# Chunkwise attention over eight heads at once: masks in the exponent matmul, exponents one half-batch ahead, row normalisation moved to ScalarE

## The reference

```python
q = layernorm(x);  k = v = ctx                         # per head
D[s,t] = exp(g[t] - max_{u<=s} g[u])  for t <= s, else 0   # g: input gate minus the summed log forget gate
C = (q @ k.T / sqrt(32)) * D
C = C / (max(|sum(C)|, exp(-m)) + 1e-6)
h = C @ v;  h = head_layernorm(h) * outnorm_weight
x = x + h
x = x + moe(layernorm(x))     # 8 experts, top 2 of them for each token, silu(h1) * h2
```

## Time and profile before

| | us |
|---|---|
| time before, median of 3 runs | 697.69 (697.56 to 697.80) |
| the profiled execution's own time | 699.08 |
| its span | 697.0 |
| TensorE busy | 599.0 |
| VectorE busy | 479.0 |
| ScalarE busy | 315.7 |
| GpSimd busy | 306.7 |

### The profile page before, as it was taken

The page is one execution under the profiler, slowest core; times in us unless marked ns, Lnnn a source line. Parts: engine busy times, 40 slices in busy tenths (PEclk is TensorE's granted clock), DMA queues, the critical chain, the costliest instruction groups (busy, mean ns, idle before and its releaser), DMA issues.

```text
span 697.0 us, 14852 instructions
## 1 busy us (share of the span) xinstructions
PE 599.0 (86%) x3480; PEld 465.8 (67%) x3481; DVE 479.0 (69%) x1039; ACT 315.7 (45%) x704; POOL 306.7 (44%) x312
## 2 busy tenths in 40 slices
PE   3874499999999997411799999999999999999993
PEld 1331266676667665311588888888888888888883
DVE  3663447778787887899367676767677676767673
ACT  2454344545445453100455555555555555555551
POOL 2223435463645545000355454555555454555532
PEclk9998599999999999555799999999999999999997
DMA  8995545556564653351132433333332333333332
GB/s 272 294 305 170 176 134 158 177 171 180 164 196 156 174 166 105 104 205 8 39 63 47 62 49 58 53 54 53 54 61 46 62 49 58 53 54 56 51 46 24
DMA packets 71673, 76.77 MB, mean 110 GB/s; under 512 B 12830, under 2 KB 63780, under 8 KB 71652
## 3 DMA queue, kind: packets, MB, share of 16 engines
q1 hardware_dynamic: 55652, 50.27, 23.0%
q0 software_dynamic: 15712, 25.73, 20.3%
q10 hardware_dynamic: 288, 0.52, 0.2%
HBM read 53.29 MB, written 23.21 MB: 110 GB/s over the span
## 4 chain that ended last, share of the span: by engine, by line
PE 71%; DVE 15%; DMA 5%; issue 3%; ACT 2%; SPq 1%; POOL 1%; DVEq 0%; ACTq 0%; POOLq 0%
PE bank L1270 10%; PE bank L1272 10%; PE bank L1271 9%; PE bank L1168 6%; PE bank L1184 6%; PE bank L1302 5%; PE bank L1298 5%; PE bank L1299 5%; PE bank L1285 4%; DMA qT_scratch<-qt 3%; PE bank L1257 2%; PE bank L1233 2%; PE bank L1165 2%; PE bank L1163 2%; DVE ohn L934 2%
## 5 line engine op out<-in xcount | busy, mean ns | idle before, releaser
L1090 POOL DMA_INDIRECT out_rows<-ys,index x71 | 113.5, 1599 | 153.7 <-DVE ys L986 145.2
L1270 PE MATMUL bank<-w12l,xh 128*128 x284 | 120.3, 424 | 2.2 <-DVE xl L958 2.2
L1272 PE MATMUL bank<-w12h,xh 128*128 x284 | 112.4, 396 | 0.0
L1271 PE MATMUL bank<-w12h,xl 128*128 x284 | 112.2, 395 | 0.0
L992 DVE TENSOR_TENSOR w3l<-w,w3h 128x1024 fp32r<-128x1024 f32 x71 | 87.2, 1228 | 31.0 <-issue 30.0
L1081 POOL DMA_INDIRECT xg<-token_table,index x71 | 70.5, 993 | 74.9 <-DVE index L951 53.0
L1184 PEld LDWEIGHTS bank<-aug,c 128*128 128x128 f32 x512 | 67.1, 191 | 29.9 <-issue 24.4
L656 ACT CAST w3h<-w 128x1024 fp32r x71 | 74.4, 1048 | 20.0 <-issue 20.0
L1298 PE MATMUL bank<-w3l,hth 128*128 128x256 f32 x284 | 76.5, 302 | 1.8 <-DVE w3l L992 1.8
L641 ACT ACTIVATE sg<-bank 128x512 f32<-128x512 f32 x71 | 42.6, 599 | 76.2 <-PE bank L1272 76.2
L782 DVE SCALAR_TENSOR_TENSOR c<-bank,d 128x512 f32<-128x512 f32 x64 | 44.1, 690 | 46.3 <-PE bank L1184 38.0
(11 more groups left out here) (164 smaller groups left out, 1087.0 us busy)
## 6 DMA issues: line engine op xcount, KB each, us to landing
x<-in_x SPq DMA_DIRECT2D x32, 256.0 KB, 3.3
wst<-in_w12T POOLq DMA_DIRECT2D x26, 256.0 KB, 3.6
aug<-in_ctxv SPq DMA_DIRECT2D x16, 264.0 KB, 3.0
ct<-in_ctxT SPq DMA_DIRECT2D x16, 256.0 KB, 4.5
qT_scratch<-qt SPq DMA_DIRECT2D x16, 256.0 KB, 3.7
kt<-in_ctxT SPq DMA_DIRECT2D x16, 256.0 KB
qbd<-qT_scratch SPq DMA_DIRECT2D x64, 64.0 KB
out_rows<-x SPq DMA_DIRECT2D x16, 256.0 KB, 2.2
```

Of the source, the lines that this page charges most:

```text
L1090: q.indirect_dma_start(out=out, out_offset=bass.IndirectOffsetOnAxis(ap=index[:, j:j + 1], axis=0), in_=YS[o][:], in_offset=None, compute_ ...
L1270: mm(acc, XH[i][:, k, :], wl, start=(k == 0), stop=False)
L1271: mm(acc, XL[i][:, k, :], wh, start=False, stop=False)
L1272: ins = mm(acc, XH[i][:, k, :], wh, start=False, stop=(k == NK - 1))
```

## The change

- The exponents and scores of a chunk cover all 8 heads: two banks each (`weighs`, `dots`), and one tile d and one tile c of two halves, where there were two tiles of one half each.
- The mask is no longer a matmul of its own. LG and RM have 92 contraction rows: 27 as before and 65 that give the mask of one half (64 queries) of a chunk. So the exponents of four heads are two matmuls of 256 columns (queries 0 to 63, 64 to 127 of each head) with different stationary operands, 8 matmuls a batch. LG is kept twice, and is loaded by two DMAs a batch. The constant rows are loaded by 6 DMAs after the gate stage; the 6 constant loads of the mask, the identity and LG/RM in the gate stage are gone.
- TensorE's order in step b: scores(b, 0), state update, transposes(b-3), exponents(b, 1), values(b, 0), scores(b, 1), carried state of b, gate scores(b-3), exponents(b+1, 0), values(b, 1). So `in3` of batch b+1 is waited for within step b.
- ScalarE's order in step b: copy of chunk 0 (b-1), `kvb`, copy `x2t` (b-3), weights(b, 1), square (b-1), power (b-2), weights(b+1, 0), Ln and Exp that give `sc` (b-1) directly, x2n (b-2) as two Identity activations with scale and bias, `high`.
- VectorE's order: joining of chunk 1 (b-1), combine(b, 0), normaliser and centring, statistics (b-2), combine(b, 1), variance, one small product (`nb3`), scores copy. The reciprocal is gone: sc = (var/32 + 1e-6 w w) to the power -1/2, w the normaliser; the minimum normaliser has 1e-6 added and is capped at 1e12 once, when `cols` is made.
- GpSimd makes `vw` of batch b+1 at the end of step b, behind the scaling of batch b-2. AUG, KN and QTB wait for `pv_group` of batch b-2.
- The loop has one turn less and two steps more behind it are written out.

In the diff, removed lines of the functions printed above are left out.

```diff
--- before.py
+++ after.py
@@ -56,6 +56,10 @@
 LN_EPS, HEAD_EPS, NORM_EPS = 1e-5, 1e-6, 1e-6
 PARTS = 3
 MASKED = -1e30
+LARGEST = 1e12
+HALF = P // 2
+GROWS = PARTS * (NH + 1)
+MROWS = GROWS + HALF + 1
...
-        bank = [stack.enter_context(nc.psum_tensor(f"bank{i}", [P, 512], F32)) for i in range(8)]
+        weighs = stack.enter_context(nc.psum_tensor("weighs", [P, 2, 512], F32))
+        dots = stack.enter_context(nc.psum_tensor("dots", [P, 2, 512], F32))
+        bank = [weighs[:, 0, :], weighs[:, 1, :], dots[:, 0, :], dots[:, 1, :]]
+        bank += [stack.enter_context(nc.psum_tensor(f"bank{i}", [P, 512], F32)) for i in range(4, 8)]
...
-            with eng.Fori(2, B // 2) as it:
+            with eng.Fori(2, B // 2 - 1) as it:
                 step(it * 2, 0)
                 step(it * 2 + 1, 1)
-            for b in range(B, B + 3):
+            for b in range(B - 2, B + 3):
                 step(b, b % 2)
...
+        LOADS3 = 1 + HG + 3
         LOADSV = 3
...
+            for i in range(2):
+                for lo, hi in ((0, PARTS), (GROWS, MROWS)):
+                    sp.dma_start(LG[i][lo:hi, :, :], lgc[lo:hi, :].rearrange("q (a s) -> q a s", a=2)
+                                 ).then_inc(mask_rows, 16)
+                sp.dma_start(RM[i][PARTS:, :, :], rmc[PARTS:, :].rearrange("q (h s) -> q h s", h=NH)
+                             ).then_inc(mask_rows, 16)
...
                     wait(sp, s_ready, 2 * NG * (b - 1))
-                    sp.dma_start(LG[i][PARTS:, :], g_dram[b].rearrange("q h s -> (q h) s")).then_inc(in3[i], 16)
+                    for a_ in range(2):
+                        sp.dma_start(LG[i][PARTS:GROWS, a_, :], g_dram[b].rearrange("q h s -> (q h) s")
+                                     ).then_inc(in3[i], 16)
...
-                    wait(sp, inter_ready, b - 1)
+                    wait(sp, pv_group, NC * (b - 1))
                     if isinstance(b, int) and b == 0:
...
@@ -574,25 +581,22 @@
                                  scale=-1.0).then_inc(dcol_ready, 1)
             pieces2(EARLY2, len(PIECES2))
+            def weights(b, c):
+                for r_ in range(2):
+                    k = (b * NC + c) * 2 + r_
+                    act.wait_ge(e_ready, k + 1)
+                    wait(act, c_ready, k - 1)
+                    nc.scalar.activation(D[:, r_, :], weighs[:, r_, :], ACT.Exp).then_inc(d_ready, 1)
...
+                if has(b, 3):
+                    act.wait_ge(x2t_psum, b - 2)
+                    wait(act, score_psum, b - 3)
+                    nc.scalar.copy(X2T[:].rearrange("p k s -> p (k s)"), bank[7][:]).then_inc(x2t_ready, 1)
+                if has(b, 0):
+                    weights(b, 1)
...
                 if has(b, 2):
                     act.wait_ge(late_steps, 2 * NC * (b - 1))
                     power(rs3[:], lnv3[:], mv3[:, :, 1], 0, var3_log, b - 1, rstd3)
+                if has(b + 1, 0):
+                    weights(b + 1, 0)
                 if has(b, 1):
                     act.wait_ge(z_ready, b)
...
+                    nc.scalar.activation(lnz[:], z[:], ACT.Ln).then_inc(z_log, 1)
+                    act.wait_ge(z_log, b)
+                    wait(act, y_done, b - 1)
+                    nc.scalar.activation(sc[:], lnz[:], ACT.Exp, scale=-0.5).then_inc(sc_ready, 1)
+                if has(b, 2):
+                    act.wait_ge(nb_ready, b - 1)
+                    for c in range(NC):
+                        ins = nc.scalar.activation(X2N[i][:, c, :], X[i][:, c].rearrange("p h d -> p (h d)"),
+                                                   ACT.Identity, bias=nb3[:, c:c + 1], scale=rs3[:, c:c + 1])
+                    ins.then_inc(x2n_ready, 1)
                 if has(b, 0):
                     high(b + B, wst[i][:], IN1 + 8 * (b - i) + 16, wst_in[i])
+            weights(0, 0)
...
+                def combine(c):
+                    for r_ in range(2):
+                        k = (b * NC + c) * 2 + r_
                         dve.wait_ge(s_ready, k + 1)
                         dve.wait_ge(d_ready, k + 1)
...
+                        wait(dve, pv_group, b * NC + c)
+                        v.scalar_tensor_tensor(C[:, r_, :], dots[:, r_, :], KS, D[:, r_, :],
                                                ALU.mult, ALU.mult).then_inc(c_ready, 1)
...
                 if post:
...
+                    dve.wait_ge(inter_ready, b)
+                    dve.wait_ge(pv_group, NC * b)
                     wait(dve, x2_ready, pb - 1)
...
                                     ALU.add).then_inc(o1_taken, 1)
+                if has(b, 0):
+                    combine(0)
                 if post:
...
+                    dve.wait_ge(o1_taken, b)
+                    dve.wait_ge(o0_taken, b)
                     sums = tot_[:, :, DH]
...
+                    v.scalar_tensor_tensor(wabs[:], sums, -1.0, sums, ALU.mult, ALU.max)
                     st.then(v.tensor_reduce(mu[:], vals, AX.X, ALU.add))
...
+                    v.scalar_tensor_tensor(wden[:].rearrange("p (c h) -> p c h", c=NC),
+                                           wabs[:].rearrange("p (c h) -> p c h", c=NC), NORM_EPS,
+                                           cols[:, 2:4, bass.ds(pb * NH, NH)], ALU.add, ALU.max)
+                    st.then(v.scalar_tensor_tensor(vals, heads(mu), -1.0 / DH, vals, ALU.mult, ALU.add))
+                    dve.sem_inc(cen_ready, 1)
+                    st.then(v.scalar_tensor_tensor(least[:], wden[:], HEAD_EPS, wden[:], ALU.mult, ALU.mult))
                 if late:
                     dve.wait_ge(x2_ready, lb + 1)
                     statistics(late_steps, lb, X[i][:].rearrange("p c h d -> p c (h d)"), st3, mv3)
+                if has(b, 0):
+                    combine(1)
                 if post:
...
+                    dve.wait_ge(sq_ready, b)
                     st.then(v.tensor_reduce(var[:], X2N[o][:].rearrange("p c (h d) -> p (c h) d", h=NH), AX.X, ALU.add))
...
+                    v.scalar_tensor_tensor(z[:], var[:], 1.0 / DH, least[:], ALU.mult, ALU.add).then_inc(z_ready, 1)
+                    assert st.n == K3, st.n
                 if late:
                     dve.wait_ge(rstd3, lb + 1)
...
+                    v.scalar_tensor_tensor(nb3[:], mv3[:, :, 0], -1.0, rs3[:], ALU.mult, ALU.mult).then_inc(nb_ready, 1)
                 if isinstance(b, int) and b == B + 2:
                     dve.wait_ge(score_ready, B - 1)
...
@@ -1070,6 +1081,9 @@
                     load_w(b + B, i, W2 - 1 + b)
                 if has(b, 1):
                     low(b - 1 + B, wst[o][:], W2 + b)
+                if has(b + 1, 0):
+                    weighted(b + 1, o)
+            weighted(0, 0)
             mixing(pool, step)
...
@@ -1151,57 +1165,52 @@
             pe.wait_ge(w_lo, W2 - len(wst))
             pe.wait_ge(late_consts, 16 * N_LATE)
+            pe.wait_ge(mask_rows, 16 * N_ROWS)
+            def exponents(b, i, c):
+                if c == 0:
+                    pe.wait_ge(in3[i], loaded(b, i, LOADS3))
+                for r_ in range(2):
+                    k = (b * NC + c) * 2 + r_
+                    wait(pe, d_ready, k - 1)
+                    for a_ in range(2):
+                        at = c * P + a_ * HALF
+                        ins = mm(weighs[:, r_, :].rearrange("p (j q) -> p j q", j=HG)[:, :, a_ * HALF:(a_ + 1) * HALF],
+                                 LG[i][:, a_, c * P:(c + 1) * P],
+                                 RM[i][:, r_ * HG:(r_ + 1) * HG, at:at + HALF],
+                                 start=True, stop=True)
+                    ins.then_inc(e_ready, 1)
+            def scores_(b, i, c):
+                wait(pe, c_ready, (b * NC + c) * 2)
+                for hg in range(NG):
+                    ins = mm(dots[:, hg, :], KT[i][:, hg, c * P:(c + 1) * P],
+                             QBD[i][:, hg, :, c * P:(c + 1) * P], start=True, stop=True)
+                    ins.then_inc(s_ready, 1)
+            def values(b, i, c):
+                pe.wait_ge(c_ready, (b * NC + c + 1) * 2)
+                if c == 0:
+                    pe.wait_ge(inv3[i], loaded(b, i, LOADSV))
+                    wait(pe, o0_taken, b)
+                else:
+                    wait(pe, o1_taken, b)
+                for h in range(NH):
+                    hg, j = h // HG, h % HG
+                    wide = min(WIDE, (NC - c) * NH - h) * DV
+                    at = (c * NH + h) * DV
+                    from_ = j * P
+                    ins = mm(bank[4 + c][:, h * DV:h * DV + wide], C[:, hg, from_:from_ + P],
+                             AUG[i][:].rearrange("p c h d -> p (c h d)")[:, at:at + wide], start=True, stop=True)
...
                     pe.wait_ge(vw_ready, b + 1)
                     wait(pe, score_ready, b - 3)
@@ -1210,19 +1219,27 @@
                         ins = mm(bank[6][:, n * HG * DV:(n + 1) * HG * DV], KN[i][:, n * P:(n + 1) * P],
```

(23 more changed lines are left out.)

## The result

The changed kernel takes 717.34 us, the median of four executions (714.54 to 720.27); the kernel before takes 697.75 us (697.56 to 698.5). The ratio is 1.028, with a 95% interval of 1.024 to 1.032: slower by 2.8%, where 2.5% faster was forecast. The profiled execution took 720.27 us with a span of 718.6; before, it was 699.08 and 697.0.

The account below looks back on a forecast made before the run. Mixing was taken as bound by TensorE's own work. Savings of 11.9 (12 steps), 4.2 (other four) and 2.2 (end), less 0.5 (start), took 17.8 off 699.08, giving 681.3; predicted median 680.0 us, range 673.5 to 692.5.

Parts of the forecast that it names:

- What bounds before: Mixing in the kernel before: bound by TensorE's own work, 12.03 us a step without a hole, 12.24 on average.
- TensorE's own new step: TensorE's work per mixing step after the change: 12.03 less 1.1 for the exponents, 10.9 us.
- Start: Before mixing: a second LG issue costs 0.5 us; the six late constant loads taken as 0, bounds 0 and +2.5.
- Exponents: TensorE in mixing: eight 256-column matmuls at 0.14 us, 1.1 a batch, a gain of 1.1 (range -0.4 to +1.3).
- Weights and columns take turns: Rival on TensorE's exponents: each matmul takes 0.23 us, 1.84 a batch, step 11.7, time 688; chance 0.06.
- The loop: Mixing: store, next loads, landing, exponents, ScalarE, x2n and store again take 11.25 us (10.8 to 12.15), setting 12 steps.
- L: Landing time of the last QBD load, 64 KB, in mixing: taken as 2.2 us, from 1.77 to 3.1.
- The late loads: End of the load queue in mixing: `vw` ready about 12.1 us after the store, costed at nothing.
- The step over all: Mixing's 12 steps with a store ahead of their loads: from 12.24 to 11.25 us each, 11.9 saved.
- The other four steps: Mixing's steps outside those 12: 1.06 us saved each, 4.2 in all.
- End: From the last values to the top 2: 12.7 us before, 2.2 saved (0 to 3).
- What I said would show it wrong: Signs in mixing: a step over 12.2 us, holes ahead of values(b, 1) ended by VectorE's c, or eight exponent matmuls over 2.

Follow-up runs that it names:

- e12: The kernel before, with exponents waiting only for gate rows and row maxima, the first scores for KT and QBD; 699.27 us, ratio 0.9994.
- e8: The kernel before with only the mask moved into the exponents' matmul, constant rows in pieces that divide; 700.08 us, ratio 1.0036.
- e4: e1's kernel with exponents waiting for LG and RM alone, the scores for KT and QBD; 684.97 us, ratio 0.9802.
- e11: e4's kernel with the mask undone, again a second matmul in the exponents; 694.72 us, ratio 0.9931.
- e2: The kernel before plus RM's constant rows loaded at the new, late place as 89 rows, twice; 724.4 us, one execution.
- e3: The kernel before plus RM's constant rows loaded at the new, late place as 96 rows, twice; 700.24 us, one execution.
- e1: The changed kernel with the constant rows of LG and RM loaded in pieces of 3, 24, 64 and 1 rows; 693.71 us, ratio 0.9938.
- e9: e4's kernel with AUG, KN and QTB of the next batch issued ahead of the store; 686.19 us, ratio 0.9805.
- e7: All computation left out, single loads of 3 to 96 rows of 4 KB timed one after another; 89 rows 15.8 us, 96 rows 3.5.
- e10: e9's kernel with the twelve loads of constant mask rows moved back into the gate stage; 686.46 us, ratio 0.9807.
- e5: e1's kernel with all loads of the next batch issued ahead of the store on SyncE; 696.91 us, ratio 0.9959.
- e6: e5's kernel with e4's edit, exponents waiting only for gate rows and row maxima; 695.41 us, ratio 0.9887.

## Why the prediction was wrong, point by point

- **What bounds before: right, but the cover behind it was thin.** TensorE is busy 58.5 of 60, and cutting the queue's loop brings nothing (e12). But e8 shows that the chain through VectorE, ScalarE and `x2t` was only 0.1 to 0.2 a step behind. TensorE's own new step, 10.9 in the forecast, is at most 10.2 to 10.4, since four steps of e4 take no longer. Of what it fell by more than forecast, 0.2 is the exponents' (below) and 0.3 was there with the old mask (11.77 in e11 for 12.03).
- **Start: wrong, and it alone turned the sign.** The failing step is "The six constant loads (0.75 MB) go out behind the gate loads, and nothing on the way to the scans' results stands behind them except the late w12 pieces": bounds 0 and +2.5, taken as 0 in the sum; measured, the start is 27.3 later. The cost was judged without the number of rows, which puts the 89-row loads on one engine (e2 against e3), and the queue was read wrong: KT, QBD, the w12 pieces and the stores of the scans all stand behind these loads. They are 848 KB, not 0.75 MB, which matters little. With rows that divide, the start is +2.9, still above the bound (e1). None of the rivals was this one. And rows 8 name GpSimd's w12l, not the landing of RM, as what the first matmul waited for.
- **Exponents: nearly right.** In the row of 198.10 above four matmuls span 0.61; one takes 0.27 at the median (0.272 of 128 in the view of the line), so they start 0.11 apart: 0.88 a batch for the eight, where I took 1.1. "Weights and columns take turns" didn't happen: each has weights of its own and no hole ahead. Of the two sums that I made from the Trainium skill ("TensorE: Matmul & The Clock Gate", sections "Back-to-back issue gap" and "LDWEIGHTS"), the one in which load and stream overlap, a gain of 1.3, agrees with 0.11 apart; the other, 1.7 a batch, does not.
- **The loop: the right mechanism, sized 0.4 too short.** Forecast 11.25, measured 11.61 in the step shown. The mis-sized term is L, 2.65 for 2.2. The queue took 5.85 for 5.98 (5.43 and 0.55 for the second LG), ScalarE 2.60 for 2.47, the way to it 0.51 for 0.6. The figure of the Trainium skill that gave 2.15 ("DMA: Bandwidth & Descriptors", "Anatomy of one DMA") stands there for loads that GpSimd issues, and these are SyncE's. e4 shows the loop by cutting it.
- **The late loads, "costed at nothing": wrong by a little in the changed kernel, and late next in e4.** `vw` came 12.16 after its store, 12.1 forecast; TensorE waited 0.40 for it in that step and 2.28 in the worst, of 13.02.
- **The step over all.** 12 x (12.25 - 11.97) = 3.4 in place of 11.9. The loop explains 0.36 of the 0.72 by which the step is too long. Most of the rest is one step of 15.25 with the low clock (below): it is 3.6 over the 11.65 of nine ordinary ones, 0.30 when spread over the twelve. The other four steps saved 3.7 for 4.2.
- **End: no gain.** I took 2.2; values to top 2 took 12.7 before and 12.7 after (293.65 to 306.31). `x2n` left VectorE but not the chain: the last scores that the top 2 starts with wait for the transposes at 302.24, and these waited 4.87 for ScalarE's Identity.
- **What I said would show it wrong** was a step over 12.2, holes ahead of the values or slow exponents. But for one hole of 1.16 ahead of values(b, 1) none came, and the step of 11.97 wasn't in the 11.0 to 11.5 that would have shown it right; the list watched only mixing and left the start out.

With rows that divide the kernel is at 693.71 (e1): the sign would have been right and the time still 1.2 above the range.

## What to carry to other kernels

Write beside each new load how many rows each side has and their largest divisor up to 16; a prime row count above 16 makes the load 4 to 5 times slower and, through the issuing queue, everything behind it, so cut it into pieces that divide, or better add rows until the count divides: each piece is an issue in the queue, twelve of them cost over 4 us here, while 96 rows at once cost next to nothing in e3 (in the changed kernel this was not tried). Let each instruction wait only for the loads that it reads, and before moving an instruction in a queue follow both ways: who stands behind it, and who waits for the buffer that it frees. When TensorE's work is cut, name the chain that is next late: the mask takes 1.3 a step off TensorE, which was worth nothing alone and 0.75 once the other engines had made room. And a wait in a trace is not yet a cause: in e9 the Square waits for a store, and the step hangs on VectorE.

## What the runs showed of the hardware

- A load of 89 rows of 4 KB runs on 1 of 16 DMA engines (a share of 0.06), at 26 to 27 GB/s in the changed kernel, and takes 15.8 us alone (e7); 88 and 90 rows take 3.7 and 3.6.
- Two such loads hold up the issue of the next ones in the same queue: KT's took 12.42 us (15.74 in e2) in place of 0.4. The loads behind were not late in landing but in being issued.
- TensorE's granted clock (1.00 is 2.4 GHz, 0.50 is 1.2 GHz) fell inside mixing in five of the traces: the changed kernel, e1, e8, e9 and e10. With TensorE busy 60 of 60 us (e11) or 58 of 60 (before) the clock is 1.00 throughout, but so it is in e5 and e6, with 52 of 60. In the changed kernel three stretches in a row are at 0.86, 0.91 and 0.81, the first two with TensorE busy 10.6 and 10.2 of 12, and the step from 165.16 to 180.41 takes 15.25. In it TensorE waits 1.75 for QBD, and the values and scores behind that wait take 3.37 and 3.76 in place of 1.93 and 1.91:

```profile
152.00:164.00 12.00, 10.64 (x66) 9.16 (x67) 5.59 (x15) 5.71 (x16) 8.03 (x12) 0.86 0.50 152
164.00:176.00 12.00, 10.24 (x64) 8.32 (x63) 8.45 (x19) 6.74 (x19) 4.76 (x7) 0.91 0.64 179
176.00:188.00 12.00, 11.98 (x64) 8.60 (x64) 8.36 (x18) 5.36 (x15) 6.11 (x9) 0.81 0.61 180
```

In e9 a dip came before batch 3's update (0.93 from 104 to 128): TensorE waits 1.74 for VectorE's `c`, and the four scores' matmuls behind it take 3.58 in place of 1.9. So a wait can cost more than its length. Which waits bring the clock down I can't say from these runs: e4 has eight, of up to 1.6, and stays at 1.00, and e1 has one of 1.89 with no dip behind it (160.95).
